# Attention over edges: a wide key-and-value addition, some values added by GpSimd, some masks made by VectorE

## What is computed

```python
q = (x @ Wq + bq).reshape(n, H, C)
k = (x @ Wk + bk).reshape(n, H, C)
v = (x @ Wv + bv).reshape(n, H, C)
e = (edge_attr @ We).reshape(-1, H, C)
kj = k[src] + e
vj = v[src] + e
logits = jnp.einsum('ehc,ehc->eh', q[dst], kj) / np.sqrt(C)
m = jax.lax.stop_gradient(jax.ops.segment_max(logits, dst, num_segments=n))
ex = jnp.exp(logits - m[dst])
denom = jax.ops.segment_sum(ex, dst, num_segments=n)
a = ex / (denom[dst] + 1e-16)
agg = jax.ops.segment_sum(vj * a[:, :, None], dst, num_segments=n)
```

## Time and profile before

| | us |
|---|---|
| median of 3 runs | 4827.8 (4825.8 to 4828.0) |
| the profiled execution, its own time | 4832.1 |
| its span, first to last instruction | 4830.3 |
| e1, first to last key addition | 1368.7 to 2917.0 |
| e2, first to last key addition | 3129.7 to 4648.3 |
| busy in the span | PE 4189.2, DVE 3989.0, ACT 2982.2, POOL 3116.4 |

### The profile page before, as it was taken

How to read it: one execution, slowest core, us unless ns; L and a number is a source line. 1 busy time by engine, 2 the same in 40 slices (tenths; PEclk the granted TensorE clock), 3 DMA queues, 4 the chain that set the end, 5 groups by cost and what they waited for, 6 DMA issues and landing times. The chain is left out here.

```text
span 4830.3 us, 107746 instructions
## 1 busy us (share of the span) xinstructions
PE 4189.2 (87%) x17694; PEld 3210.6 (66%) x17694; DVE 3989.0 (83%) x22772; ACT 2982.2 (62%) x10607; POOL 3116.4 (65%) x2996
## 2 busy tenths in 40 slices
PE   2887887888979999999999998889999999999988
PEld 2766666675547777777777774567777777777755
DVE  4655555556869999999999998789999999999986
ACT  1111111112319898989898984149999999989971
POOL 6677777740067777777777771287777777777730
PEclk9999999999999999999999999999999999999989
DMA  4666666654568887878788773587777777777734
GB/s 121 189 192 196 192 193 193 191 167 149 169 212 237 233 236 232 233 229 236 231 234 228 231 230 104 173 247 231 226 230 228 231 228 227 226 228 231 226 114 149
DMA packets 663064, 996.73 MB, mean 206 GB/s; under 512 B 99667, under 2 KB 489690, under 8 KB 662407
## 3 DMA queue, kind: packets, MB, share of 16 engines
q0 software_dynamic: 171408, 540.40, 38.1%
q1 hardware_dynamic: 491000, 449.44, 30.8%
HBM read 870.01 MB, written 119.44 MB: 205 GB/s over the span
## 5 line engine op out<-in xcount | busy, mean ns | idle before, releaser
L1303 POOL DMA_INDIRECT e_kv<-kv,src x1664 | 1635.0, 983 | 748.1 <-DVE e_kvj L1420 449.7
L1571 ACT ACTIVATE e_vals<-e_kvj,e_ex 128x65 f32<-128x65 f32 x6572 | 1725.1, 334 | 5.5 <-PE e_sum L1366 5.1
L1366 PE MATMUL e_sum<-e_vals,e_mask 128*128 128x260 f32 x3328 | 1063.7, 403 | 206.2 <-ACT e_vals L1571 190.0
L1325 PE MATMUL e_q<-q,e_pick 128*128 x3328 | 1017.2, 387 | 95.3 <-DVE e_logit L1428 66.4
L1428 DVE CUSTOM_DVE_ANT_0 e_kvj<-e_kvj,e_q 128x64 f32<-128x64 f32 x6656 | 1060.2, 214 | 3.4 <-PE e_q L1325 2.2
L152 POOL DMA_INDIRECT e_x<-x_rows,e_src x783 | 747.3, 954 | 263.1 <-issue 172.3
L1366 PEld LDWEIGHTS e_sum<-e_vals,e_mask 128*128 128x128 f32 x3328 | 563.0, 190 | 454.4 <-issue 379.7
L1325 PEld LDWEIGHTS e_q<-q,e_pick 128*128 128x128 f32 x3328 | 618.2, 191 | 252.4 <-issue 169.9
L1315 PE MATMUL e_e<-e_we,e_ea 112*128 112x256 f32 x2496 | 752.3, 382 | 17.4 <-DMA e_ea<-attr_tiles 16.2
L1316 PE MATMUL e_e<-e_we,e_ea 112*128 112x256 f32 x2496 | 745.8, 380 | 0.0
L1510 DVE TENSOR_TENSOR acc<-acc,e_sum 128x260 f32 x1664 | 697.3, 419 | 41.4 <-issue 23.6
(11 more groups left out here) (223 smaller groups left out, 4479.1 us busy)
## 6 DMA issues: line engine op xcount, KB each, us to landing
e_ea<-attr_tiles SPq DMA_DIRECT2D x1248, 112.0 KB
edges<-q SPq DMA_DIRECT2D x208, 256.0 KB
e_spots<-locals SPq DMA_DIRECT2D x416, 128.0 KB
e_made<-edges SPq DMA_DIRECT2D x416, 128.0 KB
e_kv<-kv,src POOLq DMA_INDIRECT x1664
kv<-n_proj_rows SPq DMA_DIRECT2D x98, 256.0 KB
q<-attr_tiles SPq DMA_DIRECT2D x208, 112.0 KB
n_x<-x_rows SPq DMA_DIRECT2D x98, 128.0 KB
```

The source lines that it names most:

```text
L1303: e.indirect_dma_start(out=kv[:, u, :], out_offset=None, **rows_of(kv_rows, k["src"][:, i:i + 1])).then_inc(kv_got[u], 16)
L1325: e.matmul(pe_q[i % 2][:, 0:D], pick[:, c, at:at + P], rows, start=True, stop=True).then_inc(q_done, 1)
L1366: e.matmul(sums[n % 2][:, 0:VALS], mask[:, n % R, :], vals[:, n % R, :], start=True, stop=True).then_inc(summed, 1)
L1571: by_weight = e.activation(vals[:, n % R, h * HV:(h + 1) * HV], kvj[:, 2 + n % NV, h, :], ACT.Copy, scale=ex[:, b % 2, h, r:r + 1])
```

## The change

In three of four steps the two additions of `logits` become one instruction with a 128x2x4x64 operand: keys and values at once, with the edge product read twice (a broadcast). The dot products wait for it (`kvj_done`). In the fourth step VectorE adds only the keys. GpSimd adds the values of that step (`last_values`), from `kv` and `made`, one quad later, after the gather of the next quad's last step. Gathers into that buffer, and the load of `made`, wait for it (`values_done`). The mask of steps with n % 4 == 0 is made by VectorE in one instruction between the dot products and `add_sums`, and ScalarE leaves out its two.

```diff
@@ sync, load_made
-                        e.wait_ge(vj_done, (c - 1) * QUAD)
+                        e.wait_ge(kvj_done, (c - 1) * QUAD)
+                        e.wait_ge(values_done, c - 1)
@@ gpsimd
+                def gather(i):
+                    u = i % NG
+                    if i >= NG:
+                        e.wait_ge(kvj_done, i - NG + 1)
+                        if (i - NG) % QUAD == QUAD - 1:
+                            e.wait_ge(values_done, (i - NG) // QUAD + 1)
+                    e.indirect_dma_start(out=kv[:, u, :], out_offset=None,
+                                         **rows_of(kv_rows, k["src"][:, i:i + 1])).then_inc(kv_got[u], 16)
+
+                def last_values(c):
+
+                    i = QUAD * c + QUAD - 1
+                    e.wait_ge(kv_got[i % NG], 16 * (i // NG + 1))
+                    e.wait_ge(made_got[c % 2], 16 * (c // 2 + 1))
+                    if i >= NV:
+                        e.wait_ge(weighed, i - NV + 1)
+                    by_head = "p (h c) -> p h c"
+                    e.tensor_tensor(kvj[:, 2 + i % NV, :, 0:C], kv[:, i % NG, D:].rearrange(by_head, h=H),
+                                    made[:, c % 2, :].rearrange(by_head, h=H), ALU.add).then_inc(values_done, 1)
...
                 for i in range(T):
...
+                    gather(i)
+                    if i % QUAD == QUAD - 1 and i >= QUAD:
+                        last_values(i // QUAD - 1)
+                last_values(s.quads - 1)
@@ vector, logits
-                    e.tensor_tensor(kvj[:, i % 2, :, 0:C], kv[:, i % NG, 0:D].rearrange("p (h c) -> p h c", h=H), edge,
-                                    ALU.add).then_inc(kj_done, 1)
-                    if i >= NV:
-                        e.wait_ge(weighed, i - NV + 1)
-                    e.tensor_tensor(kvj[:, 2 + i % NV, :, 0:C], kv[:, i % NG, D:].rearrange("p (h c) -> p h c", h=H), edge,
-                                    ALU.add).then_inc(vj_done, 1)
-                    e.wait_ge(kj_done, i + 1)
+                    if at < QUAD - 1:
+                        if i >= NV:
+                            e.wait_ge(weighed, i - NV + 1)
+                        e.tensor_tensor(kvj[:, key_at:value_at + 1:value_at - key_at, :, 0:C],
+                                        kv[:, i % NG, :].rearrange("p (a h c) -> p a h c", a=2, h=H),
+                                        edge.unsqueeze(1).to_broadcast([P, 2, H, C]), ALU.add).then_inc(kvj_done, 1)
+                    else:
+                        e.tensor_tensor(kvj[:, key_at, :, 0:C], kv[:, i % NG, 0:D].rearrange("p (h c) -> p h c", h=H), edge,
+                                        ALU.add).then_inc(kvj_done, 1)
+                    e.wait_ge(kvj_done, i + 1)
@@ vector, the loop
+                    if 0 <= i - LAG < T and vector_masks(i - LAG):
+                        make_mask(i - LAG)
@@ scalar
-                        if n < LATE:
+                        if not vector_masks(n):
@@ before each of ScalarE's weighings
+                        if n % QUAD == QUAD - 1:
+                            e.wait_ge(values_done, n // QUAD + 1)
```

More of the change, by code:

```diff
@@ L1183, in edge_pass_attention @@
             ph.sems("kv_got", NG), ph.sems("ea_got", NE), ph.sems("runs_got", 2), ph.sems("spots_got", 2))
-        made_got = ph.sems("made_got", 2)
+        made_got, values_done = ph.sems("made_got", 2), ph.sem("values_done")
         w_got, cleared, ones_set = ph.sem("w_got"), ph.sem("cleared"), ph.sem("ones_set")
-        e_done, q_done, kj_done, vj_done, dots_done, picked, apart_done = (
-            ph.sem(n) for n in ("e_done", "q_done", "kj_done", "vj_done", "dots_done", "picked", "apart_done"))
+        e_done, q_done, kvj_done, dots_done, picked, apart_done = (
+            ph.sem(n) for n in ("e_done", "q_done", "kvj_done", "dots_done", "picked", "apart_done"))
         flat_done, lr_done, fw_done, mx_inner = (ph.sem(n) for n in ("flat_done", "lr_done", "fw_done", "mx_inner"))
@@ L1212, in skips_added, with vector_masks, vector_masks_before @@
                 e.wait_ge(skip.added, done)
+        def vector_masks(n):
+            return n >= LATE or n % QUAD == 0
+        def vector_masks_before(n):
+            return -(-min(n, LATE) // QUAD) + max(n - LATE, 0)
         def mask_made(e, n):
-            if n < LATE:
-                e.wait_ge(masked, n + 1)
+            if vector_masks(n):
+                e.wait_ge(vector_masked, vector_masks_before(n) + 1)
             else:
-                e.wait_ge(late_masked, n - LATE + 1)
+                e.wait_ge(masked, n - vector_masks_before(n) + 1)
         def by_head(row):
@@ L1313, in edge_product @@
                     if a >= 2:
-                        e.wait_ge(vj_done, step_of(a - 2) + 1)
+                        e.wait_ge(kvj_done, step_of(a - 2) + 1)
                     e.matmul(pe_e[a % 2][:, 0:D], ea[:, a % NE, 0:P], we[:, 0, :], start=True, stop=False)
@@ L1405, in logits @@
                     e.wait_ge(kv_got[i % NG], 16 * (i // NG + 1))
+                    key_at, value_at = i % 2, 2 + i % NV
                     c, at = i // QUAD, i % QUAD
@@ L1510, in add_sums, with make_mask @@
                     e.tensor_tensor(rows, rows, sums[n % 2][:, 0:VALS], ALU.add).then_inc(added, 1)
+                def make_mask(n):
+                    if n >= R:
+                        e.wait_ge(summed, n - R + 1)
+                    e.tensor_scalar(mask[:, n % R, :], k["iota"][:], k["local"][:, n:n + 1], None, ALU.is_equal).then_inc(vector_masked, 1)
                 def late_part(n):
                     b, r, h = n // BATCH, n % BATCH + 1, H - 1
-                    e.wait_ge(summed, n - R + 1)
-                    e.tensor_scalar(mask[:, n % R, :], k["iota"][:], k["local"][:, n:n + 1], None, ALU.is_equal).then_inc(late_masked, 1)
                     e.wait_ge(ex_done, b + 1)
+                    if n % QUAD == QUAD - 1:
+                        e.wait_ge(values_done, n // QUAD + 1)
                     e.tensor_scalar(vals[:, n % R, h * HV:(h + 1) * HV], kvj[:, 2 + n % NV, h, :], ex[:, b % 2, h, r:r + 1], None,
@@ L1557, in _ @@
                         b, r = n // BATCH, n % BATCH + 1
-                        if n < LATE:
-                            if n:
-                                e.wait_ge(masked, n)
+                        made_before = n - vector_masks_before(n)
+                        if not vector_masks(n):
+                            if made_before:
+                                e.wait_ge(masked, made_before)
                             e.activation(apart[:], k["iota"][:], ACT.Square, bias=k["local"][:, n:n + 1],
                                          scale=-1.0).then_inc(apart_done, 1)
-                            e.wait_ge(apart_done, n + 1)
+                            e.wait_ge(apart_done, made_before + 1)
                         if n >= R:
                             e.wait_ge(summed, n - R + 1)
-                        if n < LATE:
+                        if not vector_masks(n):
                             e.activation(mask[:, n % R, :], apart[:], ACT.Relu, bias=k["one"][:, 0:1],
```

9 lines of the change are left out of this document (2 added, 7 removed).

## The result

The changed kernel takes 4957.4 us (median of 4, 4944.4 to 4964.3) where the kernel before takes 4826.8: 1.027 times as long, 95% interval 1.025 to 1.030. The forecast was slower, +39 us; it is slower by about 130 us, three times as much, and just inside the range, whose upper end was 4970. Beside its variants it was measured twice more: 1.0256 (1.0238 to 1.0274) and 1.0255 (1.0238 to 1.0272).

A forecast was written before the change was run, and what follows sets the result against it. VectorE was taken as the bound: its own row of instructions +54 us, contention with GpSimd +20, waits that come back -35, together +39 us on 4827.8, so 4867 us (+0.8%); range 4799 to 4970 us.

The forecast's parts named there:

- The bound: VectorE, busy 95% and 96% in stretches of e1 and e2, sets the pace before the change and after it.
- Wide addition: In three of four steps, 0.717 us against 0.665 for two additions: +0.052 us, 1248 times, +65 us.
- Keys alone: Every fourth step VectorE adds only keys: 0.449 us instead of 0.665, -0.216 us, 416 times, -90 us.
- Mask: VectorE makes the mask of every fourth step: 0.20 us of spacing each, 396 in all, +79 us.
- Own row and what comes back: VectorE's own instructions 65 - 90 + 79 = +54 us; waits for ScalarE and TensorE that go, -35 us.
- Contention with GpSimd: GpSimd's work holds up VectorE's masks: 0.05 us each, a twelfth of the upper bound of 0.6 us, +20 us.
- Rival 4: VectorE's mask waits for GpSimd's pick or new addition, 0.3 us more and not 0.05: +99, 4966 us; chance 0.11.
- Rival 3: GpSimd becomes the bound: 4979 us if its addition takes 1.3 us, 5100 us if 1.589; chance 0.12.
- The range: The measured time was to lie between 4799 and 4970 us.
- Rival 1: ScalarE's relief is worth more than its waits show: 4799 us, or about 4830 half-way; chance 0.23.
- Rival 2: The dot product's dependent start behind the wide addition costs nothing: 144 us less, 4723 us; chance 0.04.

## Why the prediction went wrong

- **The bound** held: VectorE before and after.
- **Wide addition**: 0.052 us dearer forecast, 0.715 against 0.665 measured. Held. That the wait for ScalarE moves in front of the keys was costed at nothing and was 42 us where ScalarE has no relief, in the run of the wide addition alone.
- **Keys alone**: 0.449 forecast, 0.446 without GpSimd's addition. **Mask**: 0.20 forecast, 0.205 without it. Held.
- **Own row and what comes back**: 54 - 35 = +19 us forecast without contention; without GpSimd's addition the change costs 1 us. Held within 20 us, in part by luck: the mask alone gives back 96 us and not 35, and beside the wide addition and the shorter fourth step much of that is lost again.
- **Contention with GpSimd**: this is the step that failed. "+20 us" was a twelfth of the upper bound for the mask alone; GpSimd's addition costs 123 us, of which by spacing the mask has 48, the keys 13 and instructions that the change does not touch 58. The rows were there: the scan of 0.98 us in the earlier trace rows, held up by work that GpSimd already did. I took their rarity as a fixed rate, while the change gives GpSimd a third kind of work in SBUF and VectorE a new instruction that is liable to it. And what I priced, a mask beside the work that GpSimd had already, costs nothing: 0.205 us without the addition, where 0.20 is bare. 39 + 100 = 139 us, against 130 measured.
- **Rival 4** had the mechanism and, at 4966 us, nearly the time, but booked all of it on the mask and was given 0.11. **Rival 3** did not come: GpSimd's addition took 0.75 us, and its row 7.23 us a quad (from the gather at 3807.47 to that at 3814.70), just the forecast's 6.48 + 0.75, under VectorE's 7.6; and without the addition VectorE's waits are no fewer.

```profile
3807.47 1.03 POOL L1309 DMA_INDIRECT e_kv<-kv,src  x1 [0.17 <-issue]
...
3814.70 1.03 POOL L1309 DMA_INDIRECT e_kv<-kv,src  x1 [0.17 <-issue]
```

- **The range** held, by 13 us, and by luck: what it allowed for was a dear mask or a slow GpSimd, and what came was a hold-up of many instructions.
- **Rival 1** (ScalarE worth more than its waits show) is what the mask alone does, 4807 us; in the change it is buried. **Rival 2** did not come: a dependent start costs what the scans in the earlier trace rows say, 0.715 us against 0.717.

## What to carry to other kernels

Work that is given to GpSimd is not free for VectorE, even where GpSimd has the time: here each addition of 0.75 us cost VectorE 0.28. Cost it by the time for which GpSimd reads SBUF, and count every instruction of VectorE that takes its tensors from SBUF, also those that the change leaves alone: here the masks (one tensor), keys, scans, rescaling and small factors were held up, and those with an operand in PSUM (wide additions 0.68 us, PSUM masks 0.346) were not. Before merging two instructions, look whether the second covered the wait of the first's user, and whether a wait in front of the second now holds the first. A small relief of an engine that runs close behind the bound can be worth more than its listed waits (96 us against 47 here), as each short wait also breaks the overlap of neighbours; it is best tried alone. And before a variant is read as a test of one thing, look at the waits that it needed: in the mask from PSUM a stricter wait cost some 10 us behind the passes.

## What was not expected of the hardware

A GpSimd addition of 128x256 (0.75 us) cost VectorE 118/416 = 0.28 us each. A mask that started inside it lasted 0.58 us in the mean where 0.28 is bare. Reading from PSUM made the mask 0.346 us long in all states of GpSimd, and of its 26 us of spacing only 9 were left in the passes. Writes of GpSimd in place of the addition left masks 0.33 us long in the mean, but their spacing at the bare 0.20.
